# Transposing the softmax rows of an attention kernel with VectorE and DMA instead of TensorE

## The reference

```python
k = jnp.einsum('ihd,bpd->biph', W_K, x)
q = jnp.einsum('ihd,bpd->biph', W_Q, x)
v = jnp.einsum('ihd,bpd->biph', W_V, x)
scores = jnp.einsum('biph,biqh->biqp', k, q)
...
attn = jax.nn.softmax(masked / jnp.sqrt(jnp.float32(d_head)), axis=-1)
z = jnp.einsum('biqp,biph->biqh', attn, v)
```

## Time and profile before

| | us |
|---|---|
| median of 3 runs (lowest, highest) | 880.63 (880.55, 881.56) |
| the profiled execution's own time | 880.87 |
| its span, first to last instruction | 879.1 |
| TensorE busy | 861.0 (98%) |
| VectorE busy | 658.4 (75%) |
| ScalarE busy | 562.4 (64%) |
| GpSimd busy | 251.2 (29%) |

### The profile page before, as it was taken

One profiled execution on the slowest core, in us unless ns is written; L12 is line 12 of the kernel. 1 busy time (PEld: TensorE's weight loads), 2 busy tenths in 40 slices (PEclk: granted clock), 3 DMA queues, 4 the chain that ended last, 5 costly groups with the idle time before them and its releaser, 6 DMA issues.

```text
span 879.1 us, 15317 instructions
## 1 busy us (share of the span) xinstructions
PE 861.0 (98%) x5462; PEld 774.7 (88%) x5462; DVE 658.4 (75%) x1703; ACT 562.4 (64%) x1276; POOL 251.2 (29%) x183
## 2 busy tenths in 40 slices
PE   6999999999999999999999999999999999999997
PEld 6889999999999999999999999999999888687886
DVE  4878887777777777777777777777778987877776
ACT  4665766655666666566666665566666687677874
POOL 3142222211112222111222211133104237485753
PEclk7999999999999999999999999999999999999999
DMA  6120000000000000000001100011000011112121
GB/s 242 54 97 1 25 25 26 25 1 1 1 2 25 25 25 25 2 1 1 1 26 34 39 1 1 1 44 49 1 1 1 14 61 37 61 61 73 49 101 43
DMA packets 10442, 28.63 MB, mean 33 GB/s; under 512 B 1408, under 2 KB 1568, under 8 KB 10112
## 3 DMA queue, kind: packets, MB, share of 16 engines
q1 hardware_dynamic: 9712, 25.80, 8.8%
q0 software_dynamic: 368, 1.34, 0.5%
q10 hardware_dynamic: 288, 0.53, 0.2%
HBM read 25.49 MB, written 2.17 MB: 31 GB/s over the span
## 4 chain that ended last, share of the span: by engine, by line
PE 93%; DVE 3%; ACT 2%; issue 1%; DMA 1%; POOL 0%; DVEq 0%; ACTq 0%; POOLq 0%
PE M L617 19%; PE M L618 19%; PE M L619 19%; PE S L617 7%; PE S L619 7%; PE S L618 7%; PE T L719 6%; PE T L617 2%; PE T L619 2%; PE T L618 2%; PE S L719 2%; DMA bc<-in_bcol 1%; PE M L667 1%; DVE tmp L980 1%; PE M L821 0%
## 5 line engine op out<-in xcount | busy, mean ns | idle before, releaser
L484 POOL TENSOR_TENSOR X<-X,fb 128x512 f32<-128x512 f32 x64 | 82.7, 1294 | 522.0 <-DVE fb L1045 522.0
L528 ACT ACTIVATE PB<-S,nb 128x128 f32<-128x128 f32 (+3 forms) x256 | 134.2, 536 | 117.8 <-DVE nb L1014 117.8
L1003 DVE TENSOR_TENSOR qk<-M,qk 128x512 fp32r<-128x512 f32 x128 | 88.4, 691 | 81.2 <-ACT qk L574 81.2
L1014 DVE CUSTOM_DVE_ANT_0 S<-S,cc 128x128 f32<-128x128 f32 (+3 forms) x256 | 117.3, 519 | 0.6 <-PE S L619 0.6
L617 PE MATMUL M<-hh,W 128*128 128x512 f32 x264 | 104.1, 394 | 0.7 <-DVE hl L990 0.7
L618 PE MATMUL M<-hl,W 128*128 128x512 f32 x264 | 103.6, 392 | 0.0
L619 PE MATMUL M<-hh,W 128*128 128x512 f32 x264 | 103.1, 390 | 0.0
L617 PE MATMUL S<-qk 128*128 128x128 f32 (+3 forms) x256 | 88.1, 344 | 0.0
L619 PE MATMUL M<-pth,vl 128*128 128x512 f32 (+3 forms) x256 | 82.8, 324 | 0.0
L618 PE MATMUL M<-ptl,vh 128*128 128x512 f32 (+3 forms) x256 | 82.6, 323 | 0.0
L619 PE MATMUL S<-qk 128*128 128x128 f32 (+3 forms) x256 | 82.4, 322 | 0.0
(11 more groups left out here) (185 smaller groups left out, 2438.5 us busy)
## 6 DMA issues: line engine op xcount, KB each, us to landing
stage<-in_wat SPq DMA_DIRECT2D x16, 512.0 KB, 3.9
gab<-scw SPq DMA_DIRECT2D x16, 256.0 KB, 3.3
tmp<-scw SPq DMA_DIRECT2D x16, 256.0 KB, 3.6
X<-in_x SPq DMA_DIRECT2D x4, 512.0 KB, 6.3
stage<-in_wfa SPq DMA_DIRECT2D x3, 512.0 KB, 3.5
out<-X SPq DMA_DIRECT2D x3, 512.0 KB, 2.6
X<-in_wmod SPq DMA_DIRECT2D x1, 1024.0 KB, 8.3
gab<-scr POOLq DMA_DIRECT2D x1, 1024.0 KB, 5.3
```

The source lines that it names most:

```text
L484: pool.tensor_tensor(X[:, a:a + 512], X[:, a:a + 512], fb[:, c2 * 512:c2 * 512 + 512], ALU.add).then_inc(s_y, 1)
L528: ins = act.activation(PB[:, P_OFF[i]:P_OFF[i] + w], PS[bk][:, a:a + w], ACT.Exp, bias=nb[:, i:i + 1], scale=-1.0, accum_out=sm[:, i:i + 1])
L1003: v.tensor_tensor(lo, bank(ev)[:], hi.bitcast(F32), ALU.subtract).then_inc(me, 1)
L1014: ins = v.tensor_tensor_reduce(PS[bk][:, a:a + w], PS[bk][:, a:a + w], mask[:, 512 - w:512], -INV, BIG, ALU.add, ALU.min, nb[:, i:i + 1])
```

## The change

P is no longer transposed by TensorE. In `norm`, behind the scalings, VectorE transposes P in blocks of 32x32 with five instructions (1280 columns in all) from `PB` into a new single tile `Yt`. The input is read with a step of four elements (`P_blocks`: 32 values s at a distance of 4, for each c). A 32x32 transpose leaves each block in its own quarter of the partitions, so four SBUF-to-SBUF DMAs a unit, one for each quarter of 32 partitions (160 KB each), spread them over all 128 partitions into `ptl`. They are issued by SP in a new event `tr(i+2)` at the end of iteration i, when the transposes (`s_ty`) and z(i) are done. In a new event `pt(i+1)`, ScalarE copies `ptl` to `pth` in two pieces of 640 columns and GpSimd subtracts in place (two instructions 128x640), ahead of its `wo` and `wh` work. `pth` and `ptl` are double. The tile `zt` is halved to make room, and z is written and read in another arrangement of the same size.

VectorE's transposes of unit u wait until the DMAs of unit u-1 have landed (`s_pt`), since `Yt` is single; the exponentials of the next unit wait for the transposes (`s_ty`). S, q, k and norm run one unit further ahead than before, v comes before z, the `h` events of three sequences are moved forward, and half of the gate tile is loaded after the attention.

```diff
-T_OFF = [0, 512, 1024, 896]
-T_AT = [0, 0, 0, 384]
-T_COLS = {0: (0, 512), 1: (512, 1024), 2: (1024, 1280)}
-T_ORDER = [(2, [2]), (1, [1, 3]), (0, [0])]
+T_BLK = [(0, 4), (4, 3), (8, 2), (7, 1)]
...
-            ("h", 0, 0), ("h", 0, 1), ("wh", 2), ("q", 0), ("k", 0), ("v", 0, 0), ("S", 0), ("norm", 0), ("q", 1), ("k", 1), ("v", 0, 1), ("T", 0), ("wh", 3)]
+            ("h", 0, 0), ("h", 0, 1), ("wh", 2), ("q", 0), ("k", 0), ("v", 0, 0), ("S", 0), ("norm", 0), ("q", 1), ("k", 1), ("v", 0, 1),
+            ("S", 1), ("q", 2), ("k", 2), ("norm", 1), ("tr", 0), ("tr", 1), ("pt", 0), ("wh", 3)]
     for i in range(NU):
         steps = list(fill.get(i, []))
 
         def add(*events):
             for ev in events:
                 plan.append(ev)
-                if steps and ev[0] in ("S", "q", "wo", "z", "v", "T"):
+                if steps and ev[0] in ("S", "q", "wo", "z", "v"):
                     plan.extend(steps.pop(0))
 
+        if i + 2 < NU:
+            add(("S", i + 2))
+        if i + 3 < NU:
+            add(("q", i + 3), ("k", i + 3))
+        if i + 2 < NU:
+            add(("norm", i + 2))
         if i + 1 < NU:
-            add(("S", i + 1))
-        if i + 2 < NU:
-            add(("q", i + 2), ("k", i + 2))
-        if i + 1 < NU:
-            add(("norm", i + 1))
+            add(("pt", i + 1))
         if i >= 2:
             add(("wo", i // 2 - 1, i % 2))
         add(*pre.get(i, []))
+        if i + 2 < NU:
+            add(("v", i // 2 + 1, i % 2))
         add(("z", i))
         if i + 2 < NU:
-            add(("v", i // 2 + 1, i % 2))
-        if i + 1 < NU:
-            add(("T", i + 1))
+            add(("tr", i + 2))
         plan += [ev for group in steps for ev in group]
         plan += post.get(i, [])
...
-        gab = sb("gab", 2048)
+        gab = sb("gab", 1024 + 1280)
...
                 return att.enter_context(nc.sbuf_tensor(name, [128, cols], dt))
 
+            qk = sa("qk", 2048, F32R)
+            PB = sa("PB", 1280)
             vh, vl = sa("vh", 2048, F32R), sa("vl", 2048, F32R)
-            qk = sa("qk", 2048, F32R)
-            zt = sa("zt", 4096, F32R)
-            pth, ptl = sa("pth", 1280, F32R), sa("ptl", 1280, F32R)
-            PB = sa("PB", 1280)
+            pth = [sa("pth0", 1280, F32R), sa("pth1", 1280, F32R)]
+            ptl = [sa("ptl0", 1280, F32R), sa("ptl1", 1280, F32R)]
+            zt = sa("zt", 2048, F32R)
...
-        PT = [ctx.enter_context(nc.psum_tensor(f"T{n}", [128, 512], F32)) for n in range(2)] + [PS[2]]
+        PT = [ctx.enter_context(nc.psum_tensor(f"T{n}", [128, 512], F32)) for n in range(2)]
...
+        Yt = gab[:, 1024:2304]
...
-            return zt[:, h * 1024:h * 1024 + 512], zt[:, h * 1024 + 512:h * 1024 + 1024]
+        def z_half(u, c2):
+
+            e = u % 2
+            return 2 * e + c2 if u // 2 % 2 == 0 else e + 2 * c2
+
+        def zs(u):
+            n, m = z_half(u, 0), z_half(u, 1)
+            both = zt[:].rearrange("p (s a n) -> p s a n", s=4, a=2)[:, n:m + 1:m - n]
+            return both[:, :, 0], both[:, :, 1]
+
+        def zc(u, c2, c):
+            o = z_half(u, c2) * 512 + 128 * c
+            return zt[:, o:o + 128], zt[:, o + 256:o + 384]
+
+        def P_blocks(i, j0, n):
+
+            a = P_OFF[i] + 128 * j0
+            return PB[:, a:a + 128 * n].rearrange("p (j s c) -> p j c s", s=32, c=4)
+
+        def Y_blocks(k, n):
+
+            return Yt.rearrange("p (c k r) -> p k c r", c=4, k=10)[:, k:k + 3 * n - 2:3]
+
+        def pt_block(t, j):
+
+            k, n = T_BLK[j]
+            return t[:].rearrange("p (b k r) -> p k b r", b=4, k=10)[:, k:k + n]
...
+                elif ev[0] == "tr":
+                    u = ev[1]
+                    sp.wait_ge(s_ty, u + 1)
+                    if u >= 2:
+                        sp.wait_ge(mf, use[("z", u - 2)] + 1)
+                    for b in range(4):
+                        src = Yt[32 * b:32 * b + 32, :].rearrange("p (c n) -> p c n", c=4)
+                        sp.dma_start(ptl[u % 2][:, 320 * b:320 * b + 320].bitcast(F32), src).then_inc(s_pt[u % 2], 16)
+                elif ev == ("z", NU - 1):
+                    sp.wait_ge(s_gd, 32)
+                    sp.wait_ge(s_pt[1], 64 * (NU // 2))
+                    flat = scr[1].rearrange("(o b) n -> o (b n)", o=1)
+                    sp.dma_start(gab[:, 1024:2048], flat.broadcast_to([128, 1024])).then_inc(s_gb, 16)
...
+                if ev[0] == "pt":
+                    u = ev[1]
+                    for c in range(2):
+                        s = slice(640 * c, 640 * c + 640)
+                        pool.wait_ge(s_ph, 2 * u + c + 1)
+                        pool.tensor_tensor(ptl[u % 2][:, s], ptl[u % 2][:, s].bitcast(F32),
+                                           pth[u % 2][:, s].bitcast(F32), ALU.subtract).then_inc(s_pl, 1)
...
-                        act.wait_ge(s_N, u)
+                        act.wait_ge(s_ty, u)
...
-                elif kind == "T":
+                elif kind == "pt":
                     u = ev[1]
-                    for n, (bk, _) in enumerate(T_ORDER):
-                        a, z = T_COLS[bk]
-                        act.wait_ge(s_T, 3 * u + n + 1)
-                        act.copy(pth[:, a:z], PT[bk][:, 0:z - a]).then_inc(s_ph, 1)
+                    act.wait_ge(s_pt[u % 2], 64 * (u // 2 + 1))
+                    for c in range(2):
+                        s = slice(640 * c, 640 * c + 640)
+                        act.copy(pth[u % 2][:, s], ptl[u % 2][:, s].bitcast(F32)).then_inc(s_ph, 1)
...
-                            if bk == 2:
-                                pe.wait_ge(s_pl, 3 * u - 2)
                         for i in chunks:
                             a, w = S_AT[i][1], 128 * (i + 1)
                             ins = mm3(PS[bk][:, a:a + w], lane(q, 128 * i, 128), lane(kk, 0, w), True, True)
                         ins.then_inc(s_S, 1)
-                elif kind == "T":
-                    u = ev[1]
-                    pe.wait_ge(s_N, u + 1)
-                    pe.wait_ge(s_P3, u + 1)
-                    for n, (bk, chunks) in enumerate(T_ORDER):
-                        if u > 0:
-                            pe.wait_ge(s_pl, 3 * u - 3 + n + 1)
-                        for j in chunks:
-                            a = T_AT[j]
-                            for i in range(j, 4):
-                                ins = pe.transpose(PT[bk][:, a + 128 * (i - j):a + 128 * (i - j) + 128],
-                                                   PB[:, P_OFF[i] + 128 * j:P_OFF[i] + 128 * j + 128], ident)
-                        ins.then_inc(s_T, 1)
                 elif kind == "z":
                     u = ev[1]
                     h = u % 4
                     pe.wait_ge(me, use[("v", u // 2, 1)] + 1)
                     va = (u // 2 % 2) * 1024 + (u % 2) * 128
-                    pe.wait_ge(s_pl, 3 * u + 3)
+                    pe.wait_ge(s_pl, 2 * u + 2)
                     for j in range(4):
-                        w = 512 - 128 * j
                         ins = mm3(o[:, 128 * j:512], (vh[:, va + 256 * j:va + 256 * j + 128],
                                                       vl[:, va + 256 * j:va + 256 * j + 128]),
-                                  (pth[:, T_OFF[j]:T_OFF[j] + w], ptl[:, T_OFF[j]:T_OFF[j] + w]), j == 0, j == 3)
+                                  (pt_block(pth[u % 2], j), pt_block(ptl[u % 2], j)), j == 0, j == 3)
                     ins.then_inc(mf, 1)
...
-                            ins = mm3(o[:, 256 * c:256 * c + 256], lane(zs(h), 256 * c2 + 128 * c, 128),
+                            ins = mm3(o[:, 256 * c:256 * c + 256], zc(2 * p + n, c2, c),
...
                     else:
-                        hi, lo = zs(ev[1] % 4)
-                    v.tensor_tensor(lo, bank(ev)[:], hi.bitcast(F32), ALU.subtract).then_inc(me, 1)
+                        hi, lo = zs(ev[1])
+                    src = bank(ev)[:].rearrange("p (s n) -> p s n", s=2) if kind == "z" else bank(ev)[:]
+                    v.tensor_tensor(lo, src, hi.bitcast(F32), ALU.subtract).then_inc(me, 1)
...
-                        ins = v.tensor_scalar(p, p, ri[:, i:i + 1], None, ALU.mult)
-                    ins.then_inc(s_N, 1)
-                elif kind == "T":
-                    u = ev[1]
-                    for n, (bk, _) in enumerate(T_ORDER):
-                        a, z = T_COLS[bk]
-                        v.wait_ge(s_ph, 3 * u + n + 1)
-                        v.tensor_tensor(ptl[:, a:z], PT[bk][:, 0:z - a], pth[:, a:z].bitcast(F32),
-                                        ALU.subtract).then_inc(s_pl, 1)
+                        v.tensor_scalar(p, p, ri[:, i:i + 1], None, ALU.mult).then_inc(s_N, 1)
+                    if u:
+                        v.wait_ge(s_pt[(u - 1) % 2], 64 * ((u - 1) // 2 + 1))
+                    for n, i in enumerate((1, 0, 2)):
+                        v.wait_ge(s_N, 3 * u + n + 1)
```

(37 more changed lines are left out.)

5 lines of the change are left out of this document (1 added, 4 removed).

## The result

| | before | after |
|---|---|---|
| median of the runs (lowest, highest), us | 880.59 (880.34, 881.56) | 959.18 (955.2, 963.79) |
| span of the profiled execution, us | 879.1 | 960.1 |
| TensorE busy | 861.0 | 856.7 |
| mean granted TensorE clock | 0.992 | 0.938 |

The changed kernel takes 1.0892 times as long as the kernel before, interval 1.0834 to 1.095. I had forecast 902 us, 1.024 times.

A forecast was written before the change was run, and what follows sets the result against it. TensorE was taken as the bound, before and after (10.52 to 9.42 us a plain unit). 880.9 - 70 (transposes) + 67 (queue) + 20 (other work) + 4 (ends) = 902 us; range 840 to 965.

The forecast's parts named there:

- X = 1.73: VectorE's five transposes of a unit, 1280 columns, take 1.73 us, from the slope of other VectorE instructions.
- VectorE's loop: VectorE and ScalarE per unit: 5.65 us to the scaling's end, X, and 1.83 for wo, v, z; 9.2 us.
- my own threshold (1.95 us): From X = 1.95 us on, VectorE and not TensorE sets the pace of a unit.
- the first term, -70: TensorE without its transposes (L719) saves 1.10 us in each of 64 units, from 10.52 to 9.42: -70 us.
- the pairs: Two units, one stalled by the weight load: 23.35 us in place of 18.84, twelve times.
- rival 2: VectorE's transposes take double time, X = 3.07 us, from the step of four; 965 us (940 with short landing), chance 0.27.
- the cover of 1.3 us a group: Slack before TensorE needs wo's bank: 1.3 us of stall hidden once per group, taken off the queue's cost.
- The queue, +67: In 16 iterations P's four DMAs wait in SP's queue behind GpSimd's weight subtraction and the load; VectorE stalls: +67 us.
- the four in a row: The last four weight iterations, in consecutive units: 13.9 us each against 9.42, 17 us of the queue's cost.
- Other work, +20: `h` events (10 us) and six layer norms (11 us) no longer fit VectorE's spare time: together +20 us, 10 to 28.
- Beginning and end, +4: Start waits for DMA round and first transposes, +4; end +2.5; TensorE's 3.0 us wait for `PB` goes: +4 us.

The follow-up runs named there:

- experiment 4: Changed kernel, but the drains of k (ScalarE's copy, VectorE's subtraction) write the key order, so VectorE's transposes read densely: 955.98 us, ratio 1.0872.
- experiment 10: Changed kernel with its own SP order, transposes reading with a step of two elements and eight DMAs of 80 KB in place of four: 948.42 us.
- experiment 3: Changed kernel, but TensorE reads k with the step of four and the mask's columns are reordered, so VectorE's transposes read densely: 957.07 us.
- 7: The kernel of experiment 6, with transposes reading with a step of two elements and eight DMAs of 80 KB in place of four: 861.28 us.
- Experiment 2: As Experiment 1, but SP waits for GpSimd's weight subtraction ahead of P's DMAs, and the weight load follows them: 944.25 us.
- Experiment 9: Experiment 1 plus z's subtraction behind the next S, step-of-two transposes with eight DMAs, and `h` passes (not `h2`) not waiting for GpSimd's sum in `X`: 856.50 us.
- Experiment 1: Changed kernel, only SP's list altered: P's four DMAs (`tr`) issued ahead of the wait for GpSimd's weight subtraction and the load: 903.70 us, ratio 1.0268.
- experiment 6: Experiment 1 with VectorE's z subtraction moved behind the next S, and GpSimd adding `wo` ahead of its two subtractions of P: 893.71 us, ratio 1.0144.

## Why the prediction was wrong

**Direction right, size 57 us off; the step that failed first is "I take X = 1.73".** It measured 2.66. All the rest of VectorE's loop was right: I had 5.65 + 1.83 = 7.48, and 10.1 less 2.66 is 7.44. By my own threshold (1.95 us) VectorE then sets the pace, and the first term, -70, shrinks: 64 x (10.52 - 10.1) is -27. By the sum that is 43 us of the miss; the runs show some 28 of them: 15 in the plain units, 9 in the pairs (experiment 4) and 4 in the irregular units (experiment 10). That was rival 2's mechanism, shown by experiments 3, 4 and 7 (536, 536 and 532 ns in place of 846), with a smaller X than its 3.07. Its 965 us are near the 959 measured, but not by the right sum: a lower X and larger other terms cancelled. The warning stood in the prediction: I took the slope from VectorE's dense instructions and wrote, under rival 2, that no row of this size reads with such a step. The slope (1.09 ns a column) is what dense transposes measured: (536 - 270)/256 is 1.04 ns, and with the step (846 - 359)/256 is 1.90.

**X explains most of the middle, and little of the rest.** Of the 29 us missed in the middle, 22 plain units at 0.7 us are 15, and that is what experiment 10 took back (14). It has X as forecast (404.20 to 405.87 us in its timeline, 1.67 us). The ten pairs at 24.4 us in place of 23.35 are 11. A pair is one round: 8.3 us from a reciprocal to the end of GpSimd's weight subtraction, 6.65 until the next transposes start (5.8 to 7.8, forecast 6.2), and 9.5 from there, X included, to the reciprocal that ends the pair. So X counts in it too. The eight DMAs of experiment 10 hide this, but with dense reads and the four DMAs as they were a pair takes 23.5 us in experiment 4 and 22.7 in experiment 3. The last 3 us of the 29 are the cover of 1.3 us a group that I took off and that doesn't show. In the irregular units experiment 10 took back only 3.8 of the 20 us, and at the ends none.

**The queue, +67.** Right in place (the sixteen units named), in mechanism and nearly in size: 16 waits of up to 4.9 us, 52.3 in sum, the four in a row 54.7 us against 56. Undoing it gave 55. Experiment 2 adds that 40 of the 55 are the wait for GpSimd.

**Other work, +20.** Mis-sized by 20 more. I had counted ScalarE's passes of `h` in front of VectorE but not that they wait for `X`, which GpSimd now adds 3.1 us later, behind P's subtractions: 22.7 us in eight waits. Experiment 9 took half of these waits out and the irregular units fell by 6 us. Experiment 1 took 5 off them (two of the stalls lie there) and experiment 10 4. The rest of these 20 us (layer norms, the first units, the last) I have only read, not tested.

**Beginning and end, +4.** It measured 13.5, all behind the last reciprocal, 191.5 against 177.1 us. In part this is the division and no cost: `norm` runs a unit further ahead, so more is left behind the last one (three z there, one before). Then TensorE waits 2.4 us for `fb` and 1.7 for the router's `wg`, behind a product of VectorE that takes 2.38 us beside a GpSimd subtraction, and 0.18 the other three times:

```profile
774.43 2.36 POOL L521 TENSOR_TENSOR W<-stage,W 128x1024 fp32r<-128x1024 f32 x1
774.46 2.38 DVE L933 TENSOR_TENSOR rt<-cc,rt 128x32 f32<-128x32 f32 x1
```

That looks like the lock of experiment 6, on a critical place. And the clock takes part. Around these waits, from 773.2 us on, it was at 1.2 GHz for 10.2 us, which at 2.4 GHz is an estimated 5.1 us of work; before, it stayed at 2.4 GHz in that place:

```profile
773.20:783.40 10.20, 8.49 (x38) 7.88 (x38) 8.74 (x17) 1.35 (x2) 7.58 (x6) 0.50 0.43 114
```

(The view lists the stretch, its length, the busy time of TensorE, its weight loads, VectorE, ScalarE and GpSimd, then the clock.) No run tested this phase; no version brought it under 188.6 us.

**GpSimd and ScalarE.** 1.563 us for 640 columns (forecast 1.57) and 0.72 (0.75): right. The matmuls on `pth` in runs of 32 columns cost nothing, as forecast: 395 ns for 512 columns in the second and third of the three matmuls, where the dense reads before had 393 and the scores have 389 to 397.

**Clock.** The prediction had no term for it. The mean granted clock was 0.992 before, 0.938 in the changed kernel and 0.972 in experiment 1. In the ten pairs its cost can be read: from the stalled transposes to the next reciprocal it took 9.07 us where the clock stayed at 2.4 GHz, 9.14 to 9.25 where it was at 1.2 GHz for 3.4 us of the unit, and 9.67 to 10.12 where for 6.8 us. That is 4 us in all ten, small beside the waits. Outside the pairs it was not separated from the waits around it.

## What to carry to other kernels

Before pricing a new instruction by columns, look at the step with which it reads and writes: a read with a step of 16 bytes took 1.8 times as long per column on VectorE and twice as long on TensorE, one of 8 bytes cost VectorE nothing, and having another instruction make the order only moved the cost. Put what a queue may issue at once ahead of what waits for a slow engine: one list of events for all engines is convenient, but an order of its own for SP was worth 55 us. And check an edit that is meant to isolate a cause for what it brings along: the eight DMAs of experiment 10 hid X's part in the pairs. And gains in a loop don't add: each edit is worth the distance to the next bound only, here TensorE's 9.4 us a unit.

## What the runs showed of the hardware

- A step of four fp32 elements (16 bytes) against dense: VectorE's 32x32 transpose of 384 columns 846 against 536 ns, TensorE's moving read of 512 columns 641 against 397. A step of two elements: 532. The Trainium skill, "SBUF — State Buffer", section "Door 1: The DMA port swizzle", asks for two accesses in a 16-byte line, and the runs agree with it. They don't agree with the same passage where it counts four fp32 as a free step. I had cited the first for rival 2, and gave rival 2 0.27.
- Written in groups of four elements 128 bytes apart, ScalarE's copy of 128x512 takes 1.13 us against 0.58; VectorE's subtraction, which also reads one input so, 1.09 against 0.69.
- VectorE's scalings beside a GpSimd subtraction of two SBUF inputs: three (128, 256 and 384 columns) in 2.10 us against 0.88; a product of 128x32 with two SBUF inputs in 2.38 against 0.18. Its 128x384 transpose beside GpSimd's subtraction of P (0.84 us) and its subtraction from PSUM beside that of the weights (0.69) kept their times.
- Four SBUF-to-SBUF DMAs of 160 KB from one queue are issued in 2.6 us, 0.65 apart, and one lands in 3.1 us in the median; of 80 KB in 2.3 us. A round of four has landed 5.3 us after its first issue in the median, a round of eight 6.7.
